# Linear attention stage: keys' exponentials from the turned context, row sums as a column of ones, queries normalised on GpSimd

## The reference

```
x = x + tanh(g_xattn[0]) * attn(_layernorm(x), ctx, ctx)     # stage 1, below
attn(q, k, v):          # q, k, v: (B, C=256, N=1024), 8 heads of 32 channels
    qh = softmax(q over the 32 channels of a head)
    kh = softmax(k over the 1024 positions)
    kvs = einsum('bnhd,bnhe->bhde', kh, vh)
    out = einsum('bnhd,bhde->bnhe', qh, kvs)
```

## Time and profile before

| | |
|---|---|
| median of 3 runs | 2205.26 us |
| the profiled execution | 2206.25 us, its span 2204.5 us |
| PE busy in the span | 2055.3 us (93%) |
| DVE, ACT, POOL | 1115.2, 1166.5, 627.2 us |
| first load of the NF4 stage | 181.59 us |

### The profile page before, as it was taken

How to read it: one execution, slowest core, us unless ns; L and a number is a source line. 1 busy time by engine, 2 the same in 40 slices (tenths; PEclk the granted TensorE clock), 3 DMA queues, 4 the chain that set the end, 5 groups by cost and what they waited for, 6 DMA issues and landing times. The chain is left out here.

```text
span 2204.5 us, 25816 instructions
## 1 busy us (share of the span) xinstructions
PE 2055.3 (93%) x9634; PEld 1027.0 (47%) x9634; DVE 1115.2 (51%) x1951; ACT 1166.5 (53%) x1827; POOL 627.2 (28%) x624
## 2 busy tenths in 40 slices
PE   7882999999999999999999999999857799999997
PEld 6771444444444444444444444444333455555543
DVE  6884243252524334252423425252546888888862
ACT  5666665656566565656656565655223344444420
POOL 1111221212121121212111121211234666677641
PEclk9995999999999999999999999999967899999999
DMA  5533211111111111111111121111111011111000
GB/s 193 172 120 97 69 48 54 48 50 61 49 54 48 57 52 50 54 50 53 55 55 48 49 58 53 54 48 39 70 45 57 15 39 48 48 49 43 15 30 29
DMA packets 58493, 128.37 MB, mean 58 GB/s; under 512 B 8704, under 2 KB 9344, under 8 KB 58368
## 3 DMA queue, kind: packets, MB, share of 16 engines
q1 hardware_dynamic: 58368, 126.72, 18.1%
HBM read 118.30 MB, written 8.39 MB: 57 GB/s over the span
## 5 line engine op out<-in xcount | busy, mean ns | idle before, releaser
L615 ACT ACTIVATE level<-level 128x512 f32<-128x512 f32 x924 | 581.7, 630 | 29.4
L809 PE MATMUL ps_ring<-xT_hi,gu_hi 128*128 128x512 f16 x1376 | 522.4, 380 | 2.8 <-DVE rel L736 2.8
L809 PE MATMUL ps_ring<-xT_hi,gu_lo 128*128 128x512 f16 x1376 | 522.1, 379 | 0.0
L809 PE MATMUL ps_ring<-xT_lo,gu_hi 128*128 128x512 f16 x1376 | 522.1, 379 | 0.0
L725 DVE SCALAR_TENSOR_TENSOR wt<-level,w_scale,absm 128x512 f32<-128x512 f32 x132 | 98.9, 749 | 496.9 <-ACT level L615 496.8
L744 DVE SCALAR_TENSOR_TENSOR X<-ps_ring,ffn_gain,X 128x512 f32<-128x512 f32 x352 | 260.3, 749 | 138.0 <-PE ps_ring L832 138.0
L679 POOL TENSOR_TENSOR gu_lo<-wt,gu_hi 128x512 f16<-128x512 f32 x88 | 102.8, 1168 | 767.0 <-ACT gu_hi L621 767.0
L832 PE MATMUL ps_ring<-dn_hi,hid_hi 128*128 128x512 f16 x704 | 266.9, 379 | 0.0
L832 PE MATMUL ps_ring<-dn_hi,hid_lo 128*128 128x512 f16 x704 | 266.8, 379 | 0.0
L832 PE MATMUL ps_ring<-dn_lo,hid_hi 128*128 128x512 f16 x672 | 254.6, 379 | 0.0
L809 PEld LDWEIGHTS ps_ring<-xT_hi,gu_lo 128*128 128x128 f16 x1376 | 134.6, 98 | 163.1 <-issue 1.0
(11 more groups left out here) (210 smaller groups left out, 2818.0 us busy)
## 6 DMA issues: line engine op xcount, KB each, us to landing
codes<-in_codes SPq DMA_DIRECT2D x132, 256.0 KB, 2.8
absm<-in_absmax SPq DMA_DIRECT2D x264, 128.0 KB, 3.1
X<-in_x SPq DMA_DIRECT2D x16, 512.0 KB, 4.2
c_in<-in_ctx SPq DMA_DIRECT2D x16, 512.0 KB, 5.2
cT<-in_ctxT SPq DMA_DIRECT2D x16, 512.0 KB, 3.4
xT_hi<-in_ctx SPq DMA_DIRECT2D x8, 1024.0 KB, 7.1
out<-X SPq DMA_DIRECT2D x16, 512.0 KB, 2.9
xT_hi<-in_ctx SPq DMA_DIRECT2D x16, 256.0 KB, 3.3
```

Of the source, the lines that this page charges most:

```text
L615: act.activation(level[u % 2][:], codes[u % RING][:] if k == 0 else level[u % 2][:], ACT.Prelu, bias=bias, scale=scale, alpha=alpha).then_ ...
L809: mm = pe.matmul(o[:], w[c][:, m, k, :], xx[:, k, ts], start=(q == 0), stop=(q == 3 * KD - 1))
```

## The change

- The keys' exponentials are no longer taken from c_in and transposed. The maximum of each channel, still from c_in on VectorE, is spread on TensorE by a product of `cm` (broadcast along the free axis) with the identity, so that each partition of psE's second bank has the 128 maxima in a row; ScalarE copies it to `cmx`. GpSimd subtracts it from the turned context (`less_max`, cT to ekT), and ScalarE takes the exponential in place (`keys`). The transposes of ek and the copy of ekT are gone.
- cT has 129 columns in each of its 8 blocks, the last of ones, so column 128 of the kv product is the keys' row sum; VectorE inverts it from psE.
- The turned-back reciprocals go through a ScalarE copy (rT) to SBUF, and GpSimd multiplies eq by them.
- Orders: on ScalarE rSx, eq, cmx, rT, xn, keys, xT_hi; on TensorE sums, output, maxima, rS transposes, kv, xT; on GpSimd less_max(i+1), rsqrt(i-1), the multiplication, rsqrt(i+2). SP's wait for the exponentials becomes one for the maximum.

The diff, without the declarations of semaphores:

```diff
--- before.py
+++ after.py
@@ -249,12 +249,13 @@
             return ctx.enter_context(nc.semaphore(name))
 
 
-        c_in, cT, eq, ek, ekT, xn = (sb(n, [P, D]) for n in ("c_in", "cT", "eq", "ek", "ekT", "xn"))
+        c_in, eq, ekT, xn = (sb(n, [P, D]) for n in ("c_in", "eq", "ekT", "xn"))
+        cT, cmx = sb("cT", [P, KD, P + 1]), sb("cmx", [P, P])
         kvm, rS = sb("kvm", [P, P]), sb("rS", [P, D // ROWS0])
-        rSx = ctx.enter_context(nc.sbuf_tensor("rSx", [P, D], F32))
+        rSx, rT = (ctx.enter_context(nc.sbuf_tensor(n, [P, D], F32)) for n in ("rSx", "rT"))
         st, mv, ve, rstd, nmr = sb("st", [P, 12]), sb("mv", [P, 2]), sb("ve", [P, 1]), sb("rstd", [P, 1]), sb("nmr", [P, 1])
         st2, mv2, ve2, rstd2, nmr2 = sb("st2", [P, 12]), sb("mv2", [P, 2]), sb("ve2", [P, 1]), sb("rstd2", [P, 1]), sb("nmr2", [P, 1])
-        cm, ncm, ksum, rks = sb("cm", [P, 1]), sb("ncm", [P, 1]), sb("ksum", [P, 1]), sb("rks", [P, 1])
+        cm, rks = sb("cm", [P, 1]), sb("rks", [P, 1])
 
 
         psE, psB, psO, psX = (ctx.enter_context(nc.psum_tensor(n, [P, D], F32)) for n in ("psE", "psB", "psO", "psX"))
...
@@ -289,7 +291,7 @@
                     sp.dma_start(c_in[h][:], c_d[b, h]).then_inc(ctx_in[h], 16)
 
                 def load_T(b, h):
-                    sp.dma_start(cT[h][:], io["ctxT"][b, h]).then_inc(cT_in[h], 16)
+                    sp.dma_start(cT[h][:, :, 0:P], io["ctxT"][b, h].rearrange("p (k j) -> p k j", k=KD)).then_inc(cT_in[h], 16)
 
                 for h in range(2):
                     sp.dma_start(X[:, h, :], x_d[0, h]).then_inc(x_in[h], 16)
@@ -302,7 +304,7 @@
                     sp.dma_start(gates[:, 2 * n:2 * n + 2], io[g].partition_broadcast(P)).then_inc(gates_in, 16)
                 for b in range(1, B):
                     for h in range(2):
-                        sp.wait_ge(ek_done, b * 2 + h - 1)
+                        sp.wait_ge(cmax_done, b * 2 + h - 1)
                         sp.dma_start(X[:, b * 2 + h, :], x_d[b, h]).then_inc(x_in[h], 16)
                         load(b, h)
                         sp.wait_ge(kv_mm, b * 2 + h - 1)
@@ -318,71 +320,96 @@
                     pool.wait_ge(ved, i + 1)
                     pool.tensor_tensor(rs_[h][:], ve_[h][:], mhalf[:], ALU.pow).then_inc(rsd, 1)
 
+                def less_max(i, h):
+                    pool.wait_ge(cT_in[h], (i // 2) * 16 + 16)
+                    pool.wait_ge(cmx_done, i + 1)
+                    after(pool, kv_mm, i - 1)
+                    pool.tensor_tensor(ekT[h][:].rearrange("p (k j) -> p k j", k=KD), cT[h][:, :, 0:P],
+                                       cmx[h][:].unsqueeze(1).to_broadcast([P, KD, P]), ALU.subtract).then_inc(sub_done, 1)
+
                 def step(i, h):
+                    if exists(i + 1):
+                        less_max(i + 1, 1 - h)
                     if exists(i - 1):
                         rsqrt(i - 1, 1 - h, mv2, ve2, rstd2, mv2_done, ve2_done, rstd2_done)
+                    if exists(i):
+                        pool.wait_ge(turned_done, i + 1)
+                        pool.tensor_tensor(eq[h][:], rT[:], eq[h][:], ALU.mult).then_inc(eqn_done, 1)
                     if exists(i + 2):
                         rsqrt(i + 2, h, mv, ve, rstd, mv_done, ve_done, rstd_done)
 
                 pool.memset(mhalf[:], -0.5).then_inc(const_set, 1)
                 pool.memset(res["half"][:], 0.5).then_inc(const_set, 1)
                 pool.memset(res["ones"][:], 1.0).then_inc(const_set, 1)
+                for h in range(2):
+                    pool.memset(cT[h][:, :, P:P + 1], 1.0).then_inc(ones_set, 1)
                 pool.wait_ge(const_set, 3)
                 for h in range(2):
                     rsqrt(h, h, mv, ve, rstd, mv_done, ve_done, rstd_done)
+                less_max(0, 0)
                 run(pool, step, scales_pool)
 
             @block.scalar
             def _(act):
-                def exponentials(i, h):
+                def maxima(i, h):
+                    act.wait_ge(cmb_mm, i + 1)
+                    after(act, sub_done, i - 1)
+                    act.activation(cmx[h][:], psE[:, BANK:BANK + P], ACT.Copy).then_inc(cmx_done, 1)
+
+                def queries(i, h):
                     act.wait_ge(nmr_done, i + 1)
                     after(act, out_mm, i - 1)
                     settle(act)
                     act.activation(eq[h][:], X[:, i, :], ACT.Exp, scale=rstd[h][:], bias=nmr[h][:]).then_inc(eq_done, 1)
-                    after(act, ekT_mm, i - 1)
-                    after(act, rks_done, i - 1)
-                    act.wait_ge(ncm_done, i + 1)
-                    act.activation(ek[h][:], c_in[h][:], ACT.Exp, bias=ncm[h][:], accum_out=ksum[h][:]).then_inc(ek_done, 1)
+
+                def keys(i, h):
+                    act.wait_ge(sub_done, i + 1)
+                    act.activation(ekT[h][:], ekT[h][:], ACT.Exp).then_inc(ek_done, 1)
 
                 def step(i, h):
                     if exists(i):
-                        after(act, kv_mm, i - 1)
-                        act.wait_ge(ekT_mm, i + 1)
-                        act.activation(ekT[h][:], psE[:], ACT.Copy).then_inc(ekT_done, 1)
                         after(act, rS_mm, i)
                         act.wait_ge(rS_done, i + 1)
 
                         act.activation(rSx[:].rearrange("p (n r) -> p n r", r=ROWS0), rS[h][:].unsqueeze(2).to_broadcast([P, D // ROWS0, ROWS0]),
                                        ACT.Copy).then_inc(rSx_done, 1)
                     if exists(i + 1):
-                        exponentials(i + 1, 1 - h)
+                        queries(i + 1, 1 - h)
+                        maxima(i + 1, 1 - h)
+                    if exists(i):
+                        act.wait_ge(rS_mm, i + 1)
+                        after(act, eqn_done, i)
+                        act.activation(rT[:], psB[:], ACT.Copy).then_inc(turned_done, 1)
                     if exists(i - 1):
                         after(act, xT_mm, i - 2)
                         act.wait_ge(nmr2_done, i)
                         settle(act)
                         act.activation(xn[1 - h][:], X[:, i - 1, :], ACT.Identity, scale=rstd2[1 - h][:], bias=nmr2[1 - h][:]).then_inc(xn_done, 1)
+                    if exists(i + 1):
+                        keys(i + 1, 1 - h)
                     if exists(i - 2):
                         act.wait_ge(xT_mm, i - 1)
                         settle(act)
                         act.activation(xT_hi[:, :, bass.ds((i - 2) * P, P)], psX[:].rearrange("p (k t) -> p k t", k=KD),
                                        ACT.Copy, scale=LN_SCALE).then_inc(hi_done, 1)
 
-                exponentials(0, 0)
+                queries(0, 0)
+                maxima(0, 0)
+                keys(0, 0)
                 act.wait_ge(gates_in, 32)
                 act.activation(tg[:], gates[:], ACT.Tanh).then_inc(tanh_done, 1)
                 run(act, step, scales_act)
 
             @block.tensor
             def _(pe):
+                def maxima(i, h):
+                    pe.wait_ge(cmax_done, i + 1)
+                    after(pe, cmx_done, i)
+                    pe.matmul(psE[:, BANK:BANK + P], cm[h][:].to_broadcast([P, P]), ident[:], start=True, stop=True).then_inc(cmb_mm, 1)
+
                 def step(i, h):
                     if exists(i):
-                        after(pe, kvm_done, i)
-                        pe.wait_ge(ek_done, i + 1)
-                        for k in range(KD):
-                            mm = pe.transpose(psE[:, k * P:(k + 1) * P], ek[h][:, k * P:(k + 1) * P], ident[:])
-                        mm.then_inc(ekT_mm, 1)
-
-                        after(pe, eqn_done, i)
+                        after(pe, turned_done, i)
                         pe.wait_ge(eq_done, i + 1)
                         for k in range(KD):
                             mm = pe.matmul(psB[:, k * P:(k + 1) * P], eq[h][:, k * P:(k + 1) * P], blk[:], start=True, stop=True)
@@ -394,17 +421,20 @@
                         for n in range(2):
                             mm = pe.matmul(psO[:, n * BANK:(n + 1) * BANK], kvm[1 - h][:], eq[1 - h][:, n * BANK:(n + 1) * BANK], start=True, stop=True)
                         mm.then_inc(out_mm, 1)
+                    if exists(i + 1):
+                        maxima(i + 1, 1 - h)
                     if exists(i):
-                        pe.wait_ge(ekT_done, i + 1)
-                        pe.wait_ge(cT_in[h], (i // 2) * 16 + 16 if isinstance(i, int) else (i - h) * 8 + 16)
-                        for k in range(KD):
-                            mm = pe.matmul(psE[:, 0:P], ekT[h][:, k * P:(k + 1) * P], cT[h][:, k * P:(k + 1) * P], start=(k == 0), stop=(k == KD - 1))
-                        mm.then_inc(kv_mm, 1)
-
                         pe.wait_ge(rSx_done, i + 1)
                         for k in range(KD):
                             mm = pe.transpose(psB[:, k * P:(k + 1) * P], rSx[:, k * P:(k + 1) * P], ident[:])
```

(26 more changed lines are left out.)

## The result

Four runs of the changed kernel took 2249.26 us in the median (2244.55 to 2252.65), four runs of the kernel before beside them 2205.34: a ratio of 1.0195, with a 95% interval of 1.0178 to 1.0212. The forecast was 2218.4 us with a range of 2209 to 2232. Slower was right; the time lies 31 us above the forecast and 17 above the range.

A forecast was written before the change was run, and what follows sets the result against it. VectorE was taken to bound the kernel's steps before; the new order of waits closes each at 10.65 us. 12 x 10.65 plus 11.30 gives 139.1 against 126.05, +13.1 in total: 2218.4 us, range 2209 to 2232.

The forecast's parts named there:

- The step that failed: Second layer norm: VectorE's nmr(i-1) at 5.59 us after rSx, ScalarE's xn 0.27 behind it at 5.86.
- Steps 2 to 13: Steady steps from rSx to rSx: 12 at 10.65 us each.
- Step 14: Step with the scales' squares behind its xT_hi: 8.95 + 2.35 = 11.30 us.
- rSx(2): End of the stage's start: the rSx copy of step 2 at 33.6 us, where it stood before.
- the order of waits: Queue orders close the step at 10.65 us through rstd, nmr, xn, keys' exponentials, xT_hi and xT_lo, despite less work.
- first rival: GpSimd passes stretched beside VectorE to 3.15 us: +2.4 a step, 2236 to 2245 us; chance 0.12.
- The second, the clock at 0.03: TensorE's clock falls in a pause of 2.0 us: +4 a step, 2255 us; chance 0.03.
- The third, free passes: GpSimd passes as cheap as VectorE's 1.22 us: step 9.78, 2206 us, no difference; chance 0.07.
- The fourth, faster: VectorE's freed 1.2 us comes through, TensorE sets the step at 8.4: -16, 2189 us; chance 0.07.
- the maximum's product: Added broadcast product on TensorE for the maximum: an eighth of the kv product's 1.95, 0.24 us.
- the turned context's landing: Load of cT in 1024 pieces of 512 B: 3.4 to 7 us, hidden in steady steps; 0.5 at the start.
- the signs that were named: Among them: second norm's ve right behind less_max, nmr waiting for rstd and xT_lo for xT_hi, 10.65 us between rSx.

The follow-up runs named there:

- e6_ts: Changed kernel with the offset nmr written as tensor_scalar in both layer norms, rstd a per-partition scalar; 2221.64 us, ratio 1.0068.
- e3_both: Changed kernel with GpSimd's multiplication waiting for the second norm's offset and four filler products on TensorE ahead of the rS transposes; 2222.41 us, ratio 1.0074.
- e2_fill: Changed kernel with four more identity products on TensorE ahead of the rS transposes, filling its pause; 2251.31 us, ratio 1.0202.
- e9_shortfill: e8_short plus four filler products in TensorE's pause; 2200.97 us, ratio 0.9984 to the kernel before.
- e8_short: e6_ts with both GpSimd passes cut to 32 columns, ScalarE taking the exponential of cT itself; 2211.81 us, ratio 1.0026 to the kernel before.
- b1: Changed kernel reordered on GpSimd, ScalarE and VectorE, with both norms' offsets computed on GpSimd; 2196.52 us, ratio 0.9958 to the kernel before.
- b2: b1 with the second norm's offset back on VectorE as a tensor_scalar; 2193.88 us, ratio 0.9954 to the kernel before.
- p1_stt: Kernel before, with one useless GpSimd pass over 128x1024 scratch added behind rsqrt(i-1) in each step; 2242.91 us, ratio 1.0178.
- e1_wait: Changed kernel with GpSimd's multiplication waiting until the second norm's offset is done; 2224.10 us, ratio 1.0080 to the kernel before.

## Why the prediction was wrong

**The step that failed** is "VectorE: `nmr`(i-1) at 5.59. ScalarE's xn(i-1) starts 0.27 behind it ...: 5.86." It took the offset's 0.16 from the earlier trace rows, where GpSimd had no long pass. In the new order GpSimd starts the multiplication at the very moment in which `rstd` is out, and the offset, which reads two tensors of SBUF, is not over before that pass is. The overlap of these two instructions, priced at nothing, is what the prediction had wrong; it cost 2.1 us a step. Set beside the forecast, in us from rSx (changed kernel from 100.94, e6_ts from 99.02):

| | forecast | changed kernel | e6_ts |
|---|---|---|---|
| `cmx` starts | 2.09 | 2.09 | |
| `less_max` | 2.47 to 4.67 | 2.48 to 4.66 | |
| `rstd` out | 5.55 | 5.51 | |
| multiplication | 5.50 to 7.75 | 5.47 to 7.83 | 5.48 to 7.88 |
| `nmr` ends | 5.75 | **7.85** | 5.75 |
| `xn` starts | 5.86 | **7.96** | 5.87 |
| `xT_hi` starts | 8.05 | 10.05 | |
| `xT_lo` starts | 9.08 | 11.09 | |
| next rSx | 10.65 | 12.68 | 10.59 |

Above the failed row every entry is within 0.1 us, below it each is 2.0 to 2.1 late.

**The account.** The NF4 stage's first load was forecast at 194.7 and came at 227.18, 32.5 later. Steps 2 to 13 took 189.73 - 37.45 = 152.28 instead of 127.8: 24.5. Step 14 took 13.33 instead of 11.30: 2.0. rSx(2) stood at 37.45 instead of 33.6: 3.9, of which 2.9 go with the offset's form (34.56 in e6_ts; the first one is held by `less_max`(0), 2.13 us from 12.45), and 1.0 stands in e6_ts too. The end, from rSx(15) to the load, took 24.12 instead of 21.98: 2.1. Together 32.5. In that end the kv product ran at half clock (3.65); in e6_ts it took 1.95 and the end 21.70. In e6_ts, where only the failed step is put right, load and median are 195.48 and 2221.64, against forecasts of 194.7 and 2218.4: the order of waits was right, and so "slower" was not luck. Behind the stage the profiled execution of the changed kernel gave some 7 us back (load 45.6 later, span 38.3 longer). It is the fastest of its four. The NF4 stage, from its first load to the start of its last `level` (ScalarE's expansion of the codes), took 1362.8 us (1363.7 before); the rest took 652.8 (659.2 before). That code is the same in every kernel here, and in the fourteen traces the rest takes 652.8 to 660.0, for instance 653.0 in e3_both. So the 7 us lie within that spread; where it comes from is open.

**What was overlooked in the rows of before.** The prediction weighed contention, in its first rival, and looked at VectorE's *large* instructions only; there it was right that none has two inputs in SBUF. GpSimd's passes were in fact not stretched (2.18 and 2.38). The loser was the smallest instruction of the step. The tail of the trace of before has this case, not among the rows shown: an offset of 128x2, 1.22 us long (the median of its eight is 0.15), beside a pass of GpSimd, and over 0.02 behind its end.

```profile
1648.71 1.26 POOL L1027 TENSOR_TENSOR diff<-xT_hi 128x512 f32<-128x512 f32 x1
1648.77 1.22 DVE L1406 SCALAR_TENSOR_TENSOR a_nmr<-a_mv,a_rstd 128x2 f32<-128x2 f32 x1 [1.24 <-POOL a_rstd L1007]
```

The same tail has a `tensor_scalar` that is held. `nmax`, 128x4, takes 0.17 in the 3 of its 16 executions that meet no pass of GpSimd. The other 13 start inside one, take 0.82 to 1.21, and each ends 0.02 to 0.04 behind that pass:

```profile
1681.29 0.17 DVE L1466 TENSOR_SCALAR nmax<-top 128x4 f32<-128x4 f32 x1
...
1721.10 1.26 POOL L1027 TENSOR_TENSOR diff<-xT_hi 128x512 f32<-128x512 f32 x1 [1.72 <-PE a_psE L1231]
1721.17 1.21 DVE L1466 TENSOR_SCALAR nmax<-top 128x4 f32<-128x4 f32 x1
```

So the form by itself is no remedy: the `tensor_scalar` of 128x1 was not held, the one of 128x4 was. Which difference between them decides was not tried.

The Trainium skill ("GPSIMD Engine Reference", "Key points"), which the prediction named, has the condition right: VectorE with two SBUF inputs. What was missing is what the loser pays. The Trainium skill gives the price on another page ("SBUF — State Buffer", "SBUF: two separate sides"): the shared pair of ports is locked, and whoever comes second is blocked for the whole instruction of the first. The traces agree, 2.35 us for 0.16 of work beside a pass of 2.40. By that rule, with the 0.02 of the rows above, the forecast would have had 7.75 + 0.02 for the offset's end, `xn` at 7.9 and the next rSx at 12.7; 12.68 was measured.

**The rivals.** The first (0.12) had the right kind of cause and the wrong victim; its time, 2236 to 2245, ends just short of the measured one. The second, the clock at 0.03, happened, though it had little chance: with the longer step TensorE pauses 2.72 us ahead of the rS transposes, these take 1.97 and the kv product 3.64 (1.09 and 1.95 at full speed), and 0.83 to 0.86 was granted. It costs nothing in the steps of the changed kernel, as e2_fill shows, since `nmr` waits for GpSimd anyway; that TensorE's branch would set the step at half clock, at +4, is not what happened. The third, free passes, was forecast at 9.78 a step and 2206, no difference; e9_shortfill gives 9.53 and 0.16% (0.07 to 0.25) less time, below the 0.2% that the prediction counts as a change. The step was a quarter of a us off. That holds with the filler; without it, in e8_short at a clock of 0.93, it is 0.26% more. The fourth, faster, was shut out by the order in the queues, as argued. b1 and b2 bear that out from the other side: with another order the freed time does come through.

**Sizes.** `less_max` 2.18 (2.25 forecast), the multiplication 2.36 to 2.40 (2.25), `cmx` 0.25 (0.30), the maximum's product 0.38 (0.24), the turned context's landing 4.4 (3.4 to 7). None moves the sum by more than a few tenths a step; the multiplication's does not stand on the path as long as the offset is free. Of the signs that were named, `ve` did come right behind `less_max` (105.58 against an end at 105.60), but `nmr` waited for `rstd` last in only two of steps 1 to 14 (31.99 and 144.53); in the others the kv product came later.

## What to carry over

When a long pass is moved to GpSimd, list every VectorE instruction that can fall beside it by where its *inputs* are, not by how long it is: one element a partition on the critical path paid for the whole pass, 2.35 us instead of 0.16. Put such an instruction ahead of the pass, or try a form with one tensor input (a scalar per partition for the other) and look at its length beside the pass: that was enough for 128x1 here, and the tail's 128x4 is held in spite of it. And when a step lengthens by about one pass of another engine, look for the short instruction whose end sticks to that pass's end before looking at clocks.

## What the runs showed of the hardware

- A VectorE `scalar_tensor_tensor` of 128x1 with both tensors in SBUF, started inside a GpSimd `tensor_tensor`, ended with it: 2.35 us inside 2.40, 0.83 inside the last 0.81 of 2.36, 1.84 inside 1.89. It was so with two different inputs, with the same tensor twice (p1_stt) and, at 12.45 us, beside `less_max`. `tensor_scalar` of 128x1 (0.21), `bn_stats` (1.28), the maximum of a channel (1.20) and instructions with one tensor in PSUM (`kvm` 0.35, eq 1.21) kept their length. A `tensor_scalar` of 128x4 in the tail was held as well: 0.17 alone, 0.82 to 1.21 inside a pass, 13 of 13.
- GpSimd's pass over 128x1024 f32 takes 2.18 us with one input broadcast over blocks, 2.34 to 2.42 with two full inputs, and 1.89 with the same tensor as both.
- TensorE's clock was 1.00 in steps of 10.7 us with a pause of 1.4 ahead of the rS transposes (e1_wait), and 0.83 to 0.86 in steps of 12.7 with a pause of 2.7. It was 0.93 in e8_short, with a pause of 2.05 and steps of 9.53 and 11.17, and 1.00 in e9_shortfill, with the filler and steps of 9.53.
- The turned context in 1024 pieces of 512 B landed in 4.4 us, where the rows of 4 KB took 3.4; SP's issue took 0.55 us.
